# The order of a slot in the first layer's loop: bias rows and the older gradient product first, transposes after the state products

## Chip, cores and metric

The kernel runs on one core of a Trainium2 chip. The metric is the device time of one execution in microseconds, the median of the runs shown. TensorE multiplies matrices and writes PSUM; VectorE and ScalarE compute elementwise and read and write PSUM and SBUF; GpSimd computes elementwise in SBUF only. Each engine takes its instructions strictly in the order written for it, and waits at a semaphore hold up all that stands behind them.

## What is computed

Two transformer layers over 4 sequences of 512 tokens, 128 wide. The change touches the attention part of the first layer only, a test-time-training recurrence: 16 heads of width 64, 8 chunks of 64 tokens, and in each chunk and head

```python
Z1 = xk_c @ W + bb
x_hat = (Z1 - mu) / std
y = g * x_hat + be
gxh = (y - (xv_c - xk_c)) * g
grad_x = (HD * gxh - gxh.sum(-1) - x_hat * (gxh * x_hat).sum(-1)) / (HD * std)
Wn, bn = W - (eta * xk_c).T @ grad_x, bb - (eta * grad_x).sum(-2)
Zq = xq_c @ Wn + bn
out = xq_c + g * ((Zq - mu2) / std2) + be
```

so a chunk needs the weights W and the bias bb that the chunk before has left. Behind it follow the first layer's mixture of experts and the whole second layer, which the change leaves as they are.

## The kernel before

The kernel is written as one stream per engine, with counted semaphores between them. The recurrence is a loop of 38 slots, `for s in range(4 * NC + 6)` (L533 on ScalarE, L821 on VectorE, L1294 on TensorE; GpSimd has its own, L1083). A chunk is four slots: slot s holds chunk s // 4, one half of the heads (s % 4 // 2) and one pair of sequences (s % 2). Slots 0 to 31 compute Z and its gradient; slots 4 to 35 compute Zq of the chunk before, so in slots 4 to 31 both run side by side. I call s % 4 the kind of a slot.

TensorE's parts of a slot, in the words used below: **bias_rows** (L1178) puts the bias into the two PSUM banks that hold Z and Zq; **state_q** and **state** (L1187) add the products of queries and keys with the weights, 64x64 tiles; **XK_** (L1229) transposes the keys into `second_bank`; **target** (L1217, then L1135 to L1137) computes the gradient's constant part into `first_bank`; **bias** (L1250, odd slots only) subtracts two slots' gradients from the bias; **queries** and **keys** (L1135 to L1137) compute a piece of the next chunk's projections, in `second_bank` and `first_bank`; **dW** (L1265) is the gradient product of an earlier slot; **turn** (L1280) transposes normalised Zq of an earlier slot; **att** (L1291) is the output projection, in slots whose number less two has kind 2 or 3, that is in slots of kind 0 and 1.

ScalarE's parts: **squares** (L476) of Z, **squares_q** (L512) of Zq, **deviation** (L481) and **deviation_q** (L517), both square roots, **bias_high** (L507), and the copies out of PSUM **take_xk** (L491), **take_turned** (L524), **take_u** (L486), **take_queries** (L501), **take_att** (L530), **take_keys** (L457).

VectorE's parts: sums of squares (L747, L809), reciprocals (L753, L814), **xhat** (L759), **normed** (L819, the normalised Zq), **bias_low** (L797), **gradient** (L773), **sum_gx** (L779), **sum_gx_xhat** (L791), **centre** (L785), **update** (L804, weights less dW's product). GpSimd's **scaled** (L1055) follows xhat; **rated** (L1081) ends the gradient.

What ties them around the change: Z and Zq have one PSUM buffer each, so bias_rows of slot s + 1 waits for xhat and for normed of slot s (L1172 and L1174) and, every second slot, for bias_low. normed(s) needs deviation_q(s), which stands behind take_queries(s) in ScalarE's order (L537). queries(s) waits until take_xk(s) has emptied `second_bank`. dW has one PSUM buffer, emptied by update. state(s) needs the update of slot s - 4.

Of the kernel before, what the change touches and what calls it, by code (L numbers as in the profile page):

```python
# [63 lines left out]
def build(nc, A, out, const_d, dbg=None):  # L64
    with ExitStack() as ctx:
# [358 lines left out]
        def _(act):  # L424
# [46 lines left out]
            def squares(s):  # L471
                if s in LIVE:
                    act.wait_ge(CHUNK["z_ready"], s + 1)
                    if s >= 4:
                        act.wait_ge(CHUNK["zq_ready"], s - 3)
                    act.activation(by_pair(sqz[:, :]), z_of, ACT.Square).then_inc(CHUNK["z_squared"], 1)  # L476

            def deviation(s):
                if s in LIVE:
                    act.wait_ge(CHUNK["z_sumsq"], s + 1)  # L480
                    act.activation(sm[:, s % 4, 1, :], sm[:, s % 4, 0, :], ACT.Sqrt, bias=C("ttt_eps"), scale=1.0 / HD).then_inc(CHUNK["z_dev"], 1)  # L481

            def take_u(s):
                if s in LIVE:
                    act.wait_ge(CHUNK["u_ready"], s + 1)
                    act.activation(U[:, s % 4, :], first_bank[:, :], ACT.Copy).then_inc(CHUNK["u_taken"], 1)  # L486

            def take_xk(s):
                if s in LIVE:
                    act.wait_ge(CHUNK["xk_ready"], s + 1)  # L490
                    act.activation(XK[:, s % 4, :], second_bank[:, :], ACT.Copy).then_inc(CHUNK["xk_taken"], 1)  # L491

            def take_keys(s):
                if 2 <= s <= 4 * NC - 3:
                    keys((s - 2) % 4, keys_through(s), first_bank)

            def take_queries(s):
                if 2 <= s <= 4 * NC + 1:
                    m = (s - 2) % 4
                    act.wait_ge(CHUNK["queries_ready"], queries_through(s))  # L500
                    act.activation(qT[:, 2 * m:2 * m + 2, :, :].rearrange("p a b c -> p (a b c)"), second_bank[:, :], ACT.Copy).then_inc(CHUNK["queries_taken"], 1)  # L501
# [7 lines left out]
            def squares_q(s):  # L509
                if s in AFTER:  # L510
                    act.wait_ge(CHUNK["zq_ready"], s - 3)
                    act.activation(by_pair(sq2[:, :]), zq_of, ACT.Square).then_inc(CHUNK["zq_squared"], 1)  # L512

            def deviation_q(s):
                if s in AFTER:
                    act.wait_ge(CHUNK["zq_sumsq"], s - 3)
                    act.activation(rq[:, s % 4, 1, :], rq[:, s % 4, 0, :], ACT.Sqrt, bias=C("ttt_eps"), scale=1.0 / HD).then_inc(CHUNK["zq_dev"], 1)  # L517

            def take_turned(s):
                if s in AFTER:  # L520
                    if s == 4:
                        act.wait_ge(wog_ready, 1)
                    act.wait_ge(CHUNK["normed_turned"], s - 3)
                    act.activation(AT[:, s % 4, :], misc[:, :], ACT.Copy).then_inc(CHUNK["turned_taken"], 1)  # L524

            def take_att(s):
                if s in AFTER and s % 4 >= 2:
                    j, g = s // 4 - 1, s % 2
                    act.wait_ge(CHUNK["att_ready"], 2 * j + g + 1)
                    act.activation(attnT[:, :].rearrange("p (b s) -> p b s", b=B)[:, 2 * g:2 * g + 2, j * K:(j + 1) * K],  # L530
                                   misc[:, 0:P].rearrange("p (b s) -> p b s", b=2), ACT.Identity, bias=bo0[:, :]).then_inc(CHUNK["att_taken"], 1)

            for s in range(4 * NC + 6):  # L533
                take_xk(s), take_turned(s - 2), squares(s), squares_q(s), take_u(s)
                if s % 2:
                    bias_high((s - 3) // 2)
                deviation(s), take_queries(s), deviation_q(s), take_att(s - 2), take_keys(s)  # L537
                if s == 0:
                    act.wait_ge(wq_turned, 1)
                    for n in range(2):  # L540
                        act.activation(wqT[:, 4 * n:4 * n + 4, :], bank[n][:, :].rearrange("p (a c) -> p a c", a=4), ACT.Copy).then_inc(wq_turned_taken, 1)
                if s == 1:
                    act.wait_ge(choice_step, 2)
                    act.activation(rkp[:, 1, :], lgt[:, :], ACT.Exp, bias=es[:, 0:1], accum_out=es[:, 1:2]).then_inc(choice_exp, 1)
                if s == 2:
                    act.wait_ge(out_weights, 1)
                    act.activation(Wqo[:, :], misc[:, 0:P], ACT.Copy).then_inc(out_weights_taken, 1)
                    act.activation(bo0[:, :], misc[:, P:P + 1], ACT.Copy).then_inc(out_weights_taken, 1)
                if s == 4:
                    act.wait_ge(ranks_turned, 1)  # L550
                    act.activation(rpT[:, :, :, :], misc[:, :].rearrange("p (k t r) -> p k t r", k=2, t=NT), ACT.Copy).then_inc(ranks_taken, 1)
# [91 lines left out]
        def _(dve):  # L643
# [124 lines left out]
            def gradient(s):  # L768
                if s in LIVE:
                    u = s % 4  # L770
                    dve.wait_ge(CHUNK["scaled_ready"], s + 1)
                    dve.wait_ge(CHUNK["u_taken"], s + 1)
                    dve.tensor_tensor(gx[:, u, :], t1[:, u, :], U[:, u, :], ALU.add).then_inc(CHUNK["gx_ready"], 1)  # L773
# [42 lines left out]
            def normed(s):  # L816
                if s in AFTER:
                    dve.wait_ge(CHUNK["zq_rdev"], s - 3)
                    dve.tensor_tensor(by_pair(Am[:, s % 2, :]), zq_of, per_pair(rq[:, s % 4, 2, :]), ALU.mult).then_inc(CHUNK["normed_ready"], 1)  # L819

            for s in range(4 * NC + 6):  # L821
                centre(s - 1), sum_squares(s), sum_squares_q(s), rdev(s), xhat(s), rdev_q(s)
                if s % 2:
                    bias_low((s - 3) // 2)
                normed(s), rate_of(s - 1), gradient(s), update(s - 2), sum_gx(s), sum_gx_xhat(s)
                if s == 0:
                    choice(0), choice(1)
                elif s == 1:
                    choice(2), choice(3)
                elif s == 2:  # L830
                    choice(4), choice(5)
                elif s == 3:
                    choice(6)
# [291 lines left out]
        def _(pe):  # L1125
# [166 lines left out]
                    pe.matmul(to, Wqo[:, :], xnT[:, :].rearrange("p (b s) -> p b s", b=B)[:, 2 * g:2 * g + 2, j * K:(j + 1) * K], start=False, stop=True, skip_group_check=True).then_inc(CHUNK["att_ready"], 1)  # L1292

            for s in range(4 * NC + 6):  # L1294
                XK_(s), bias_rows(s), state_q(s), state(s), target(s)
                if s % 2:
                    bias((s - 3) // 2)
                queries(s), att(s - 2), keys(s), dW(s - 2), turn(s - 1)
                if s == 0:
                    pe.wait_ge(wg_ready, 1)  # L1300
                    pe.wait_ge(rates_biased, 1)
                    for b in range(B):
                        last = pe.matmul(misc[0:BE, :], wgP[:, b, :], xnT[:, b * S:(b + 1) * S], start=(b == 0), stop=(b == B - 1))
                    last.then_inc(choice_logits, 1)
                    pe.wait_ge(wq_loaded, 16)
                    for a in range(NP):
                        last = pe.transpose(bank[a // 4][:, a % 4 * P:(a % 4 + 1) * P], wq[:, a * P:(a + 1) * P], ident)
                    last.then_inc(wq_turned, 1)
                if s == 2:
                    pe.wait_ge(wo_loaded, 16 * 5)  # L1310
                    pe.wait_ge(wq_turned_taken, 2)
                    pe.wait_ge(choice_step, 1)
                    for a in range(NP):
                        pe.matmul(misc[:, 0:P], wqT[:, a, :], wo[:, a, :], start=(a == 0), stop=(a == NP - 1))
                    for a in range(NP):
                        last = pe.matmul(misc[:, P:P + 1], wo[:, a, :], bet[:, a:a + 1], start=(a == 0), stop=(a == NP - 1))
                    last.then_inc(out_weights, 1)
                if s == 4:
                    pe.wait_ge(ranks_ready, 2)
                    pe.wait_ge(out_weights_taken, 2)  # L1320
                    for k in range(2):
                        for t in range(NT):
                            last = pe.transpose(misc[:, (k * NT + t) * BE:(k * NT + t + 1) * BE], rkp[:, k, t * P:(t + 1) * P], ident[0:BE, 0:BE])
                    last.then_inc(ranks_turned, 1)
# [255 lines left out]
```

## Time and profile before

| | us |
|---|---|
| median of 3 runs (lowest, highest) | 975.94 (974.56, 976.08) |
| the profiled execution, its own time | 973.86 |
| its span in the trace | 971.7 |
| the 38 slots of the loop, roughly | 45 to 327 of the span |
| mean granted TensorE clock | 0.973 of full |

| engine | busy us | share of the span |
|---|---|---|
| TensorE, matmul | 889.8 | 92% |
| VectorE | 786.3 | 81% |
| GpSimd | 626.3 | 64% |
| TensorE, weight load | 618.2 | 64% |
| ScalarE | 556.4 | 57% |

The shares are means over stages with different limits. A matmul's end is modelled, so the busy time of TensorE overlaps itself; the distance from one start to the next is the safer reading.

### The profile page before, as it was taken

How to read it: one execution, taken by the hardware profiler on the slowest of the kernel's cores; microseconds unless marked ns; L12 is line 12 of the kernel's file. 1: busy time of each engine (PE TensorE's matmuls, PEld its weight loads, DVE VectorE, ACT ScalarE, POOL GpSimd, SP SyncE). 2: the span in 40 equal slices, each digit the busy share in tenths (PEclk: the TensorE clock that was granted, in tenths of full speed). 3: DMA queues.
4: the chain of work that ended last, by engine and by line, in shares of the span. 5: the costliest groups of instructions: out<-in, count | busy, mean ns of one | idle time of the engine just before them, and what ended most of it. 6: DMA issues, size and time to landing. Idle time of an engine off the chain costs nothing.

```text
span 971.7 us, 19701 instructions
## 1 busy us (share of the span) xinstructions
PE 889.8 (92%) x7768; PEld 618.2 (64%) x7768; DVE 786.3 (81%) x1182; ACT 556.4 (57%) x828; POOL 626.3 (64%) x571
## 2 busy tenths in 40 slices
PE   1788999999998897799999999999999999999997
PEld 1566778778786677556666656655656666666554
DVE  7768988899886626797888897898788788888876
ACT  3444566666654362456657556666665765656653
POOL 4357888888784002868559559657757855955862
PEclk9888999999999899799999999999999999999999
DMA  8100000000000302101101111101201210220110
GB/s 228 25 2 1 2 3 2 3 2 2 3 3 1 88 2 87 39 38 64 56 12 60 65 27 62 63 4 61 73 25 55 64 47 24 70 75 20 45 52 21
DMA packets 24963, 38.26 MB, mean 39 GB/s; under 512 B 9316, under 2 KB 15480, under 8 KB 22824
## 3 DMA queue, kind: packets, MB, share of 16 engines
q1 hardware_dynamic: 23240, 34.74, 11.7%
q10 hardware_dynamic: 1632, 2.27, 0.7%
q8 instruction: 62, 1.02, 0.4%
q14 instruction: 29, 0.24, 0.1%
HBM read 28.29 MB, written 1.43 MB: 31 GB/s over the span
## 4 chain that ended last, share of the span: by engine, by line
PE 54%; POOL 18%; DVE 13%; issue 8%; ACT 5%; DMA 1%; SPq 0%; POOLq 0%; ACTq 0%; DVEq 0%
PE bank L1135 9%; POOL hdl L1108 8%; PE bank L1137 8%; PE bank L1136 8%; PE bank L1399 5%; POOL hdh L1106 4%; PE bank L1291 3%; PE quad L1187 2%; DVE hdh L954 2%; PE quad L1440 2%; POOL arena L1061 2%; POOL arena L1055 2%; PE quad L1178 2%; PE bank L1250 2%; PE quad L1335 2%
## 5 line engine op out<-in xcount | busy, mean ns | idle before, releaser
L947 DVE TENSOR_REDUCE mx<-quad 128x4 f32<-128x2048 f32 x64 | 146.4, 2287 | 41.3 <-PE quad L1430 41.2
L1106 POOL CAST hdh<-xn 128x512 fp32r<-128x512 f32 x96 | 65.6, 683 | 144.9 <-ACT xn L616 144.9
L631 ACT ACTIVATE ex<-quad 128x2048 f32<-128x2048 f32 x64 | 120.6, 1884 | 51.7 <-PE quad L1440 51.6
L1108 POOL TENSOR_TENSOR hdl<-hd,hdh 128x512 fp32r<-128x512 f32 x96 | 129.5, 1349 | 7.7
L1108 POOL TENSOR_TENSOR hdl<-xn,hdh 128x512 fp32r<-128x512 f32 x96 | 128.4, 1338 | 7.7
L616 ACT ACTIVATE hd<-bank,b1c 128x512 f32<-128x512 f32 x128 | 88.0, 687 | 64.4 <-POOL hdl L1108 30.3
L1135 PE MATMUL bank<-hdh,W2h 128*128 128x512 f32 x256 | 110.9, 433 | 3.0 <-DVE hdl L957 1.5
L616 ACT ACTIVATE xn<-bank,b1c 128x512 f32<-128x512 f32 x128 | 87.9, 687 | 33.9 <-PE bank L1137 16.5
L1137 PE MATMUL bank<-hdl,W2h 128*128 128x512 f32 x256 | 100.5, 393 | 0.0
L1136 PE MATMUL bank<-hdh,W2l 128*128 128x512 f32 x256 | 100.3, 392 | 0.0
L1135 PE MATMUL bank<-cH,W1h 128*128 128x512 f32 x192 | 81.2, 423 | 0.7 <-DVE cL L974 0.7
L1137 PE MATMUL bank<-cL,W1h 128*128 128x512 f32 x192 | 75.8, 395 | 0.0
L1136 PE MATMUL bank<-cH,W1l 128*128 128x512 f32 x192 | 75.6, 394 | 0.0
L1106 POOL CAST hdh<-hd 128x512 fp32r<-128x512 f32 x96 | 69.8, 727 | 0.0
L1135 PEld LDWEIGHTS bank<-hdh,W2h 128*128 128x128 f32 x256 | 47.9, 187 | 33.4 <-issue 12.4
L1399 PE MATMUL bank<-ex,Vx 128*32 128x512 f32 x512 | 65.1, 602 | 0.0
L969 DVE TENSOR_TENSOR cur<-cur,add 128x512 f32<-128x512 f32 x60 | 57.0, 949 | 2.1
L1061 POOL TENSOR_TENSOR arena<-arena 128x512 f32<-128x512 f32 x32 | 41.0, 1280 | 27.2 <-DVE arena L773 27.2
L963 DVE SCALAR_TENSOR_TENSOR add<-bank,b2T,cwB 128x512 f32<-128x512 f32 x64 | 47.7, 746 | 13.1 <-PE bank L1137 12.9
L1055 POOL TENSOR_TENSOR arena<-arena,gg 128x512 f32<-128x512 f32 x32 | 40.8, 1275 | 24.0 <-DVE arena L759 24.0
L1137 PEld LDWEIGHTS bank<-hdl,W2h 128*128 128x128 f32 x256 | 48.0, 188 | 11.2
L1136 PEld LDWEIGHTS bank<-hdh,W2l 128*128 128x128 f32 x256 | 48.2, 188 | 6.7
(301 smaller groups left out, 2200.4 us busy)
## 6 DMA issues: line engine op xcount, KB each, us to landing
cwB<-gate_rows SPq DMA_DIRECT2D x16, 1024.0 KB, 4.7
kx<-kqh SPq DMA_DIRECT2D x32, 64.0 KB, 2.1
qx<-kqh SPq DMA_DIRECT2D x32, 64.0 KB, 2.1
ex<-in_L_ffn_W SPq DMA_DIRECT2D x1, 1024.0 KB, 5.9
kx<-kql SPq DMA_DIRECT2D x16, 64.0 KB, 2.1
qx<-kql SPq DMA_DIRECT2D x16, 64.0 KB, 2.1
rec<-rec_rows SPq DMA_DIRECT2D x32, 32.0 KB, 2.1
out<-fin SPq DMA_DIRECT2D x4, 256.0 KB, 2.3
```

The source lines that it names most:

```text
L616: act.activation(tile(n), bank[TILE_BANK[n % 3]][:, :], ACT.Gelu_apprx_tanh, bias=b1c[:, n:n + 1]).then_inc(ROUND["gelu_ready"], 1)
L631: act.activation(ex[:, t % 2, :, :], quad[:, :, :], ACT.Exp, scale=float(AD) ** -0.5).then_inc(ROUND["exps_ready"], 1)
L947: dve.tensor_reduce(mx[:, t, :], quad[:, :, :], AX_X, ALU.max, negate=True).then_inc(ROUND["score_max"], 1)
L969: dve.tensor_tensor(now, before, add[:, e % 2, :], ALU.add).then_inc(ROUND["cur_added"], 1)
L1055: pool.tensor_tensor(t1[:, u, :], xh[:, u, :], gg[:, 512 * hf:512 * hf + 512], ALU.mult).then_inc(CHUNK["scaled_ready"], 1)
L1061: pool.tensor_tensor(t1[:, u, :], gx[:, u, :], xh[:, u, :], ALU.mult).then_inc(CHUNK["gx_xhat"], 1)
L1106: pool.tensor_copy(hdh[:, m % RING, :], tile(n)).then_inc(ROUND["pool_split"], 1)
L1108: pool.tensor_tensor(hdl[:, m % RING, :], tile(n), hdh[:, m % RING, :], ALU.subtract).then_inc(ROUND["pool_split"], 1)
L1135: pe.matmul(to, lh, rh, start=start, stop=False, skip_group_check=True)
L1136: pe.matmul(to, ll, rh, start=False, stop=False, skip_group_check=True)
L1137: return pe.matmul(to, lh, rl, start=False, stop=stop, skip_group_check=True)
L1399: last = pe.matmul(bank[5][32 * h:32 * h + 32, :], Vx[:, t, QH * r + h, :], ex[:, t % 2, h, :], start=(t == 0), stop=(t == NT - 1), skip_g ...
```

## The change

It permutes calls in the three loops; no instruction is added, removed or resized, and GpSimd's loop stays.

- TensorE: XK_ stood ahead of bias_rows and now stands behind the state products. dW of two slots back stood at the end of the slot; now dW of three slots back stands behind bias_rows, ahead of the state products. turn of one slot back stood at the end; now turn of two slots back stands between the state products and XK_. One slot has thus bias_rows, dW, state_q, state, turn, XK_, target, (bias), queries, att, keys.
- ScalarE: take_xk and take_turned stood ahead of squares, in the order named; now they follow squares and squares_q, take_turned first. deviation moves from behind bias_high to ahead of it.
- VectorE: sum_gx moves ahead of update.

```diff
@@ ScalarE
-                take_xk(s), take_turned(s - 2), squares(s), squares_q(s), take_u(s)
+                squares(s), squares_q(s), take_turned(s - 2), take_xk(s), take_u(s), deviation(s)
                 if s % 2:
                     bias_high((s - 3) // 2)
-                deviation(s), take_queries(s), deviation_q(s), take_att(s - 2), take_keys(s)
+                take_queries(s), deviation_q(s), take_att(s - 2), take_keys(s)
@@ VectorE
-                normed(s), rate_of(s - 1), gradient(s), update(s - 2), sum_gx(s), sum_gx_xhat(s)
+                normed(s), rate_of(s - 1), gradient(s), sum_gx(s), update(s - 2), sum_gx_xhat(s)
@@ TensorE
-                XK_(s), bias_rows(s), state_q(s), state(s), target(s)
+                bias_rows(s), dW(s - 3), state_q(s), state(s), turn(s - 2), XK_(s), target(s)
                 if s % 2:
                     bias((s - 3) // 2)
-                queries(s), att(s - 2), keys(s), dW(s - 2), turn(s - 1)
+                queries(s), att(s - 2), keys(s)
```

## Rows read from the trace of the kernel before

**Rows 1.** The page, part 4: shares of the chain that ended last, by engine.

```profile
PE 54%; POOL 18%; DVE 13%; issue 8%; ACT 5%; DMA 1%; SPq 0%; POOLq 0%; ACTq 0%; DVEq 0%
```

**Rows 2.** Windows: stretch, length, each engine's busy us, granted clock, DMA share, GB/s.

```profile
175.00:200.00 25.00, 25.00 (x473) 20.36 (x472) 22.36 (x41) 15.31 (x33) 20.20 (x17) 1.00 0.01 2
```

**Rows 3.** Timeline, slot 10 (kind 2): start us, length us, engine, line, operation.

```profile
130.43 0.73 PE L1178 MATMUL quad<-Bhl,pair 4*128 4x512 f32 x2
...
131.09 1.16 PE L1187 MATMUL quad<-Wst,arena 64*64 64x64 f32 x64
...
132.18 0.50 PE L1217 MATMUL bank<-gbr,ones 128*128 128x512 f32 x1
132.32 0.60 ACT L476 ACTIVATE arena<-quad 128x512 f32<-128x512 f32 x1 [0.69 <-PE quad L1187]
...
132.81 0.59 ACT L512 ACTIVATE arena<-quad 128x512 f32<-128x512 f32 x1
...
133.21 0.28 PE L1135 MATMUL bank<-xth,wqh 128*128 128x256 f32 x1
...
134.12 0.60 ACT L501 ACTIVATE arena<-bank 128x512 f32<-128x512 f32 x1
...
134.97 0.69 PE L1265 MATMUL quad<-arena 64*64 64x64 f32 x32
...
135.30 0.69 DVE L819 TENSOR_TENSOR arena<-quad,rq 128x512 f32<-128x512 f32 x1
...
135.59 0.66 PE L1280 MATMUL bank<-cst,arena 128*128 128x128 f32 x4
...
136.08 0.60 PE L1229 MATMUL bank<-cst,arena 128*128 128x128 f32 x4
```

**Rows 4.** Timeline, slot 11 (kind 3), and the first row of slot 12.

```profile
136.61 0.73 PE L1178 MATMUL quad<-Bhl,pair 4*128 4x512 f32 x2
...
139.65 1.05 PE L1250 MATMUL bank<-arena,cst 128*32 128x512 f32 x4
...
140.64 0.39 PE L1135 MATMUL bank<-xth,wqh 128*128 128x256 f32 x1
...
141.65 0.60 ACT L501 ACTIVATE arena<-bank 128x512 f32<-128x512 f32 x1
...
143.20 0.68 DVE L819 TENSOR_TENSOR arena<-quad,rq 128x512 f32<-128x512 f32 x1
...
144.02 0.70 PE L1178 MATMUL quad<-Bhl,pair 4*128 4x512 f32 x2
```

**Rows 5.** Timeline, starts of slots 8 and 9 (kinds 0, 1), parts of slot 9.

```profile
113.37 0.70 PE L1178 MATMUL quad<-Bhl,pair 4*128 4x512 f32 x2
...
121.29 0.73 PE L1178 MATMUL quad<-Bhl,pair 4*128 4x512 f32 x2
...
123.04 0.50 PE L1217 MATMUL bank<-gbr,ones 128*128 128x512 f32 x1
...
124.17 1.05 PE L1250 MATMUL bank<-arena,cst 128*32 128x512 f32 x4
...
126.22 0.60 ACT L501 ACTIVATE arena<-bank 128x512 f32<-128x512 f32 x1
...
128.08 0.69 DVE L819 TENSOR_TENSOR arena<-quad,rq 128x512 f32<-128x512 f32 x1
```

**Rows 6.** Timeline, bias_rows of slots 5, 6 and 7, with the wait ahead.

```profile
90.66 0.70 PE L1178 MATMUL quad<-Bhl,pair 4*128 4x512 f32 x2 [0.82 <-DVE arena L819]
...
98.92 0.70 PE L1178 MATMUL quad<-Bhl,pair 4*128 4x512 f32 x2 [0.44 <-DVE arena L819]
...
105.36 0.70 PE L1178 MATMUL quad<-Bhl,pair 4*128 4x512 f32 x2 [0.21 <-DVE arena L819]
```

**Rows 7.** Windows of 1 us about the clock's fall near 298; columns as in group 2.

```profile
296.00:297.00 1.00, 0.12 (x2) 0.00 (x0) 1.00 (x2) 0.60 (x1) 1.00 (x1) 1.00 0.00 0
...
299.00:300.00 1.00, 1.00 (x7) 1.00 (x6) 0.80 (x3) 0.31 (x1) 1.00 (x2) 0.50 0.00 0
```

## Prediction

> **What bounds the kernel now.** I read the page's chain first: TensorE holds 54% of it [rows 1], and only the first layer's loop, some 280 us of the 971.7, is touched. Then the windows of that loop: in 175 to 200 TensorE is busy 25.00 of 25.00 us at full clock [rows 2]. The reader should not stop there, since a queue can be full and yet only just in time. So I read the timeline of four slots, one of each kind. From one bias_rows to the next, slots 8 to 11 take 7.92, 9.14, 6.18 and 7.41 us (113.37, 121.29, 130.43, 136.61, 144.02), together 30.65 [rows 3 to 5]. The start-to-start distances in slot 10 add up without a hole: TensorE's work sets these slots.
>
> The second thing to read is when VectorE's normed comes, because bias_rows of the next slot waits for it. In slot 10 normed starts at 135.30; bias_rows can follow a normed's start by 0.82 (143.20 to 144.02 in slot 11, where it was indeed waited for), so from 136.12; it starts at 136.61 [rows 3, 4]. The margin is 0.49 us in kind 2 and nothing in kind 3. And before the loop settles, the wait is plain: bias_rows of slots 5, 6 and 7 stood idle 0.82, 0.44 and 0.21 us, released by normed [rows 6]. So this is a loop in balance: TensorE's work on one side, and on the other the chain bias_rows, products, target, (bias), queries, take_queries, deviation_q, reciprocal, (bias_low), normed, next bias_rows. What kept the chain covered is that dW, turn and XK_ stood behind keys, between the last step that the chain needs and the bias_rows that waits for it.
>
> **The change part by part.** TensorE's three moved parts, from slot 10: dW takes 0.62 (134.97 to 135.59), turn 0.49, XK_ 0.53 (136.08 to 136.61 of slot 11) [rows 3, 4]. Together 1.64 us leave the stretch where TensorE did useful work while normed was under way, and enter the stretch between bias_rows and queries, on which normed depends. Their work is the same; their place lengthens the chain by what they take and removes the cover by the same amount.
>
> For dW next to the state products the trace has no row. Bounds: 0.62 as it stands, or at the products' own rate, 64 matmuls in 1.09 us (131.09 to 132.18), so 32 in 0.55 [rows 3]. I take 0.55, because both groups are 64x64 tiles with the same count of columns; a saving of 0.07 a slot. The Trainium skill (TensorEngine Tiling (Array Packing), Key Properties) says that changing the tiling mode drains TensorE, which speaks for this change, as dW and the products would share one change of mode. The rows allow no more than that 0.07 for it.
>
> The chain by kind, with T = 0 at bias_rows. The products start at 0.66 + 0.55 = 1.21 (bias_rows takes 0.66, 130.43 to 131.09), turn at 2.30, XK_ at 2.79, target at 3.32 [rows 3].
>
> ScalarE next. squares starts 0.14 after the products give way (132.18 to 132.32), so at 2.44; ScalarE starts one such operation every 0.49 (132.32 to 132.81), so squares_q is at 2.93, take_turned 3.42, take_xk 3.91, done with 0.60 at 4.51 [rows 3]. queries may start about 0.09 later, 4.60, while TensorE is ready at 3.32 + 1.03 = 4.35 (132.18 to 133.21) [rows 3]. This is an added wait: 0.25 in even slots, with queries, att, keys queued behind it; in odd slots bias fills it. Bounds 0 to 0.25; I take 0.25, since it follows from ScalarE's order.
>
> Kind 2: queries 4.60, take_queries 0.91 later (133.21 to 134.12) at 5.51, normed 1.18 later (134.12 to 135.30) at 6.69, next bias_rows 0.82 later: **7.51** against 6.18 [rows 3, 4].
>
> Kind 3: bias at 3.32 + 1.13 = 4.45 (123.04 to 124.17; in slot 11 it waited for GpSimd's rated, which is long done now), queries 0.99 later (139.65 to 140.64) at 5.44, take_queries 1.01 later at 6.45, normed 1.55 later (141.65 to 143.20) at 8.00, next bias_rows: **8.82** against 7.41 [rows 4, 5]. The upper bound of the step from take_queries to normed is slot 9's 1.86 (126.22 to 128.08) [rows 5]; there xhat lay in between on VectorE. Now deviation stands ahead of bias_high, xhat is out of the way by then, and I take 1.55.
>
> Kind 0: att (about 1.9 us) stands behind queries and covers the chain of 7.51. TensorE's own work remains: 7.92 less 0.07 plus 0.25, **8.10**. Kind 1: 9.14 less 0.07, **9.07**; its chain of 8.82 is covered.
>
> The rest I cost at nothing. deviation(s) now follows take_u(s), which waits for a target that comes 1.6 us later; it starts at about 5.1 and xhat ends at about 6.4, ahead of normed in both kinds, so what hides it is the chain itself. If that cover went, xhat and then normed would move by the difference. update(s) waits for a dW behind bias_rows; sum_gx fills that on VectorE, and three slots remain until the weights are needed. take_xk and take_turned held nobody up. DMA: no transfer is issued in the loop's body. The first slots 0 to 4 are set by VectorE (its long selection of experts' tokens sits there), so the longer TensorE stretch hides. In slots 32 to 35 no keys and no target are left: dW and turn only change slots.
>
> Sum: four slots 33.50 against 30.65, so +2.85, six times for slots 8 to 31: 17.1. Slots 5, 6 and 7 took 8.26, 6.44 and 8.01 (90.66, 98.92, 105.36, 113.37) [rows 5, 6] and become 8.82, 7.51, 8.82: +2.4. Together **+19.5 us**: span 971.7 to 991.2, the profiled execution 973.86 to 993.4, and, since that execution lies 2.08 under the median, the median 975.94 to **995.4**.
>
> Own range of this case. Low: no wait for take_xk, giving 7.85, 9.07, 7.26 and 8.82, so +2.35 a period, 14.1 and 2.1 for slots 5 to 7: 992.1. High: dW at 0.62 and 1.86 before normed in odd slots, giving 8.17, 9.20, 7.58 and 9.20, so +3.5 a period, 21.0 and 3.3: 1000.2.
>
> **The rivals.**
>
> A. TensorE's work is all that counts (the other side). If normed comes early enough in spite of the longer way, slots remain set by TensorE, whose work is unchanged but for the 0.07 a slot, 32 times: 2.2 us, so 973.7. The skill's rule on the drain named above would be its reason and could make it more. It decides from the point where the chain of kind 2 is under 6.1 and that of kind 3 under 7.3. For it: busy 25.00 of 25.00 [rows 2]. Against: zero margin in slot 11 and waits in slots 5 to 7 [rows 4, 6].
>
> B. The clock falls. At 296 TensorE was idle for most of a microsecond, with smaller holes in the 7 us before, and from 299 to 302 it was granted 0.50, that is 1.2 in place of 2.4 GHz [rows 7]. The case above opens holes of 1.3 to 1.5 us in kinds 2 and 3 of every period. If each period then has one stretch of about 3.2 us at half clock, and half of it is lost on TensorE's path (1.6 us), seven periods cost 11 more: 1006.6. Against: slots 5 and 6 had holes of 0.82 and 0.44 and kept full clock.
>
> C. The chain shortens elsewhere. deviation ahead of bias_high and ScalarE's free time let normed come about 0.5 us sooner than I put it in kinds 2 and 3 (13 slots), and the wait for take_xk vanishes (7 slots by 0.25): 8.3 less, 987.1.
>
> **How the numbers follow.** The main case 0.54 (992 to 1000), A 0.10 (of which 0.07 faster, 0.03 within the bound), B 0.22 (1000 to 1010), C 0.14 (978 to 992, 0.01 of it within the bound). A measurement of this kernel tells 0.2%, about 2 us, from no change. So faster 0.07, same 0.04, slower 0.89. For the range, A falls outside and so does a part of C: 984 to 1010 holds about 8 in 10.
>
> **What would show it.** Right: in the middle of the loop TensorE's busy share drops to about 90%, bias_rows of kinds 3 and 0 (behind slots of kind 2 and 3) show idle time of about 1.3 and 1.4 us released by normed L819, none of that size ahead of kinds 1 and 2, and a period of 33.5 us between equal kinds. dW to the products: 0.55. queries of even slots start 4.6 us after bias_rows. B: granted clock 0.5 in some 1 us windows between 115 and 290. Wrong: a period of 30.7 or less (A), or holes released by anything other than normed, such as xhat or update, which would mean that I missed the wait that ends last.

## The result, and the profile after

| | before | changed |
|---|---|---|
| median, us (lowest, highest) | 975.25 (974.42, 976.08) | 1000.99 (997.88, 1002.24) |
| profiled execution, us | 973.86 | 1001.21 |
| its span, us | 971.7 | 999.1 |
| mean granted clock | 0.973 | 0.957 |

The ratio is 1.0253, with a 95% interval of 1.0234 to 1.0272: 25.7 us slower where 995.4 was forecast. The page's engine shares and the chain by engine, to be held against [rows 1]:

```profile
PE 891.0 (89%) x7768; PEld 624.2 (62%) x7768; DVE 783.0 (78%) x1182; ACT 551.1 (55%) x828; POOL 625.7 (63%) x571
...
PE 56%; POOL 14%; DVE 13%; issue 8%; ACT 7%; DMA 1%; SPq 0%; POOLq 0%; ACTq 0%; DVEq 0%
```

The busy times are those of before within 2 us for TensorE and 6 for any engine. Nothing got more expensive; the time is waiting. Where, is told by the windows (slot 11, then a piece of slot 12) and by the view of waits over 120 to 300 us. Columns of windows as in [rows 2]; a line of waits gives engine, its line, the releaser, total us, times, longest. PE is TensorE's matmuls, PEld its weight loads.

```profile
141.00:150.00 9.00, 6.82 (x126) 4.92 (x127) 7.67 (x16) 4.63 (x10) 6.81 (x6) 1.00 0.01 2
152.50:155.00 2.50, 2.50 (x26) 2.34 (x19) 2.24 (x4) 1.79 (x4) 2.42 (x3) 0.53 0.00 0
```

```profile
PE quad L1178 <- DVE arena L819: 14.6, 10, 1.7
...
PEld bank L1135 <- ACT arena L491: 14.1, 19, 0.8
...
PEld quad L1178 <- DVE Bhl L797: 9.4, 5, 1.9
...
PE bank L1135 <- ACT arena L491: 1.6, 7, 0.2
```

TensorE, 25.00 of 25.00 us busy in [rows 2], has holes now. bias_rows (L1178) waits for normed (L819) and for bias_low (L797), and queries (L1135) for take_xk (L491). A weight load counts as idle while matmuls ahead of it still run, so the two PE lines are the ones that give lost time: the 9.4 us of PEld behind bias_low lie in the same holes as PE's wait for normed (ahead of slot 12, 1.88 and 1.70 us), and normed, which stands behind bias_low on VectorE, ends last. In the view of before over the same stretch the wait for normed came twice, 0.4 us and, ahead of slot 32, 1.2 us, and the wait for take_xk not at all. The timeline of slot 10, which answers [rows 3]:

```profile
134.16 0.70 PE L1178 MATMUL quad<-Bhl,pair 4*128 4x512 f32 x2
...
134.79 0.69 PE L1265 MATMUL quad<-arena 64*64 64x64 f32 x32
...
135.30 1.11 PE L1187 MATMUL quad<-Wst,arena 64*64 64x64 f32 x64
...
136.34 0.66 PE L1280 MATMUL bank<-cst,arena 128*128 128x128 f32 x4
...
136.84 0.60 PE L1229 MATMUL bank<-cst,arena 128*128 128x128 f32 x4
...
137.19 0.48 PE L1217 MATMUL bank<-gbr,ones 128*128 128x512 f32 x1
...
137.93 0.62 ACT L491 ACTIVATE arena<-bank 128x512 f32<-128x512 f32 x1
...
138.60 0.39 PE L1135 MATMUL bank<-xth,wqh 128*128 128x256 f32 x1 [0.23 <-ACT arena L491]
...
139.61 0.60 ACT L501 ACTIVATE arena<-bank 128x512 f32<-128x512 f32 x1 [0.40 <-PE bank L1137]
...
140.66 0.69 DVE L819 TENSOR_TENSOR arena<-quad,rq 128x512 f32<-128x512 f32 x1
...
141.50 0.70 PE L1178 MATMUL quad<-Bhl,pair 4*128 4x512 f32 x2 [1.22 <-DVE arena L819]
```

Read it downwards as the chain: TensorE reaches queries 4.44 us after bias_rows, where it was 2.78 in [rows 3]; take_queries, normed and the next bias_rows hang on it, and TensorE idles 1.22. Slot 11, answering [rows 4], does the same and ends in a hole of 1.70:

```profile
145.65 1.05 PE L1250 MATMUL bank<-arena,cst 128*32 128x512 f32 x4
...
146.63 0.39 PE L1135 MATMUL bank<-xth,wqh 128*128 128x256 f32 x1
...
147.65 0.60 ACT L501 ACTIVATE arena<-bank 128x512 f32<-128x512 f32 x1 [0.31 <-PE bank L1137]
...
149.20 0.68 DVE L819 TENSOR_TENSOR arena<-quad,rq 128x512 f32<-128x512 f32 x1
...
150.02 0.70 PE L1178 MATMUL quad<-Bhl,pair 4*128 4x512 f32 x2 [1.70 <-DVE arena L819]
```

The holes have a second price. In the windows above the clock granted from 152.5 to 155 is 0.53, that is mostly 1.2 GHz in place of 2.4. Four of the six slots of kind 0 in the loop's middle (8, 12, 16, 20) take 9.15 us, the other two 8.09 and 8.08; slot 31 takes 11.49 where its kind takes 8.52. Slot 6 is at half clock too, from 100 to 103, and takes 8.53 where its kind takes 7.34.

Where the difference of the two spans lies, by the starts of bias_rows and of the last att:

| stretch | before | changed | more |
|---|---|---|---|
| up to slot 5 | 90.66 | 90.74 | 0.1 |
| slots 5 to 7 | 22.71 | 25.42 | 2.7 |
| slots 8 to 31 | 183.95 | 203.98 | 20.0 |
| of these: full clock, six periods of 32.80 for 30.65 | | | 12.9 |
| of these: half clock, 4 times 1.06, and 2.97 in slot 31 | | | 7.2 |
| slots 32 to the last att | 27.35 | 29.98 | 2.6 |
| from there to the first hidden activation of layer two | 73.52 | 72.79 | -0.7 |
| the second layer | 573.5 | 576.2 | 2.7 |

The 2.7 us of slots 5 to 7 hold 1.2 us of half clock in slot 6. The 2.7 us of the second layer lie in code that the change doesn't touch. In the traces of the twelve experiments the same code takes 573.3 to 575.8 us and does not follow the length of the slots, so this row is scatter between executions; it is part of why this profiled pair differs by 27.4 and the medians by 25.7.

### The profile page after: what moved, and what is told of

Same layout as the page of the kernel before. It is cut to its first block, busy times and chain, and to the rows that moved or that the text cites. A ratio compares the mean times of both kernels' runs of the same rounds, so it can differ in the third digit from the quotient of the medians.

```text
span 999.1 us, 19701 instructions
## 1 busy us (share of the span) xinstructions
PE 891.0 (89%) x7768; PEld 624.2 (62%) x7768; DVE 783.0 (78%) x1182; ACT 551.1 (55%) x828; POOL 625.7 (63%) x571
## 4 chain that ended last, share of the span: by engine, by line
PE 56%; POOL 14%; DVE 13%; issue 8%; ACT 7%; DMA 1%; SPq 0%; POOLq 0%; ACTq 0%; DVEq 0%
PE bank L1135 10%; POOL hdl L1108 8%; PE bank L1137 8%; PE bank L1136 8%; PE bank L1399 5%; POOL hdh L1106 4%; PE quad L1187 3%; PE bank L1291 3%; PE quad L1178 2%; PE quad L1265 2%; PE quad L1440 2%; PE bank L1280 2%; PE quad L1430 2%; PE quad L1335 2%; ACT ex L631 2%
## 5 line engine op out<-in xcount | busy, mean ns | idle before, releaser
L1135 PE MATMUL bank<-hdh,W2h 128*128 128x512 f32 x256 | 110.8, 433 | 2.4 <-DVE hdl L957 1.5
L1135 PE MATMUL bank<-cH,W1h 128*128 128x512 f32 x192 | 81.2, 423 | 0.7 <-DVE cL L974 0.7
L1135 PEld LDWEIGHTS bank<-hdh,W2h 128*128 128x128 f32 x256 | 47.9, 187 | 32.7 <-issue 12.4
L476 ACT ACTIVATE arena<-quad 128x512 f32<-128x512 f32 x32 | 19.1, 598 | 80.5 <-PE quad L1187 80.5
L1178 PE MATMUL quad<-Bhl,pair 4*128 4x512 f32 x72 | 27.4, 462 | 36.1 <-DVE arena L819 28.2
L963 DVE SCALAR_TENSOR_TENSOR add<-bank,b2T,cwB 128x512 f32<-128x512 f32 x64 | 47.7, 746 | 13.1 <-PE bank L1137 12.9
```

The costliest lines, as they stand in the source:

```text
L963: dve.scalar_tensor_tensor(out=add[:, e % 2, :], in0=bank[6 if e % 2 else 4][:, :], scalar=b2T[:, e:e + 1], in1=cwB[:, e, :], op0=ALU.add, ...
L1135: pe.matmul(to, lh, rh, start=start, stop=False, skip_group_check=True)
L1178: pe.matmul(quad[:, 2 + h, :].rearrange("p (q a c) -> p q a c", q=2, a=4), pair[r, :], rows[:, h].unsqueeze(1).broadcast_to([4, 2, 4, HD]) ...
```

## The experiments

Every kernel's slot lengths are read off its own timeline as distances of bias_rows starts, full-clock slots of the middle. This table is the measure of all runs:

| kernel | kind 0 | 1 | 2 | 3 | period | median us |
|---|---|---|---|---|---|---|
| before | 7.92 | 9.14 | 6.18 | 7.41 | 30.65 | 975.3 |
| changed | 8.09 | 8.85 | 7.34 | 8.52 | 32.80 | 1001.0 |
| e1, dW alone | 7.65 | 9.31 | 6.31 | 8.01 | 31.28 | 981.3 |
| e2, transposes with ScalarE | 8.23 | 8.95 | 6.90 | 8.05 | 32.13 | 989.2 |
| e3, ScalarE and VectorE alone | 9.24 | 9.27 | 7.25 | 7.39 | 33.15 | 991.9 |
| e4, changed, holes filled | 8.06 | 8.85 | 7.35 | 8.51 | 32.77 | 991.3 |
| e5, changed, deviation_q first | 8.07 | 8.79 | 7.02 | 7.62 | 31.50 | 982.5 |
| e6, changed, take_xk first | 7.60 | 8.85 | 7.01 | 8.51 | 31.97 | 995.7 |
| e7, dW ahead of bias_rows | 7.84 | 9.47 | 6.04 | 7.78 | 31.13 | 978.9 |
| e8, e7 with keys ahead of att | 8.79 | 9.71 | 6.04 | 7.78 | 32.32 | 985.3 |
| e9, e5 and e6 together | 7.59 | 8.79 | 7.04 | 7.62 | 31.04 | 979.8 |
| e10, both roots ahead of take_u | 7.60 | 8.79 | 6.56 | 8.02 | 30.97 | 983.9 |
| e11, e10, sums ahead of centre | 7.59 | 8.79 | 6.68 | 7.78 | 30.84 | 982.1 |
| e12, one dW in four moved | 7.18 | 9.61 | 6.18 | 7.41 | 30.38 | 974.5 |

**One part of the change at a time (e1, e2, e3).** The theory was the balance of the prediction; the rivals were that TensorE's work alone counts, and that one single part carries the loss.

e1:

```diff
-                XK_(s), bias_rows(s), state_q(s), state(s), target(s)
+                XK_(s), bias_rows(s), dW(s - 3), state_q(s), state(s), target(s)
-                queries(s), att(s - 2), keys(s), dW(s - 2), turn(s - 1)
+                queries(s), att(s - 2), keys(s), turn(s - 1)
-                gradient(s), update(s - 2), sum_gx(s)
+                gradient(s), sum_gx(s), update(s - 2)
```

> Only dW moves (three slots back, behind bias_rows), with VectorE's sum_gx ahead of update; turn, XK_ and ScalarE's order stay as before. Theory (balance of work and chain): in the changed kernel dW and the products run 0.15 us shorter a slot than before (dW 0.62 to 0.52, products 1.09 to 1.04), and the chain from bias_rows to normed grows by 0.52. Kinds 0 to 3: 7.8, 9.0, 6.2 and 7.75 against 7.92, 9.14, 6.18 and 7.41, together about 30.7 against 30.65, so 975 to 978 us. Rival (only TensorE's work counts): 0.15 less in each of some 30 slots, 971 us. Rival (dW's new place is the cause of the whole loss): 995 or more.

981.33 us, ratio 1.0055 (1.0039 to 1.0072), above the 975 to 978 expected. Kinds 0 and 2 came within 0.15 of the expectation; 3 and 1 came longer by 0.26 and 0.31. For kind 1 the timeline shows a wait that I had not listed: with dW gone from between keys and the transposes, XK_ of the next slot stands waiting for take_keys.

```profile
130.18 0.66 PE L1229 MATMUL bank<-cst,arena 128*128 128x128 f32 x4 [0.23 <-ACT arena L457]
...
131.42 0.69 PE L1265 MATMUL quad<-arena 64*64 64x64 f32 x32
...
131.94 1.11 PE L1187 MATMUL quad<-Wst,arena 64*64 64x64 f32 x64
...
132.98 0.51 PE L1217 MATMUL bank<-gbr,ones 128*128 128x512 f32 x1
```

The same rows show the gain that is real: dW 0.52 and the products 1.04. In kind 0, where att covers everything, the slot is 0.27 shorter.

Outside the table, slots 19 and 20 of this trace are 1.3 and 1.2 us longer than their kinds, at full clock; TensorE stands still there for 1.57 and 0.89 us without a releaser in the profile, so the cause is open.

e2:

```diff
-                XK_(s), bias_rows(s), state_q(s), state(s), target(s)
+                bias_rows(s), state_q(s), state(s), turn(s - 2), XK_(s), target(s)
-                queries(s), att(s - 2), keys(s), dW(s - 2), turn(s - 1)
+                queries(s), att(s - 2), keys(s), dW(s - 2)
```

and ScalarE in the order of the change.

> turn and XK_ go behind the state products and ScalarE follows as in the change; dW and VectorE stay as before. Theory: the chain grows by the two transposes (about 0.85) and in even slots queries waits some 0.4 us for take_xk. Kinds 0 to 3: 8.15, 9.0, 6.9 and 8.0, together +1.4 a period, about 985 us. Rival (the transposes carry the whole loss): 1000 us. Rival (TensorE's work alone): 972 us.

989.24 us, ratio 1.0134 (1.0119 to 1.0149). Each kind is within 0.08 us of what the chain gave. The total is 4 us above the 985 expected; slots 5 and 31, both partly at half clock, are 2.7 and 1.6 us longer than slot 5 of before and slots of kind 3 here. The hole ahead of slot 11 has the releaser that it should:

```profile
140.40 0.46 PE L1178 MATMUL quad<-Bhl,pair 4*128 4x512 f32 x1 [0.60 <-DVE arena L819]
```

e3 takes ScalarE's and VectorE's orders of the change, and TensorE's of before.

> TensorE's order as before; ScalarE and VectorE in the order of the change. Theory: take_xk is now done only about 4.0 us after bias_rows while TensorE is ready for queries at 2.8, so in even slots queries and all behind it wait 1.2 us; in odd slots bias covers all but 0.2. Kinds 0 and 2 grow by 1.2 each, 1 and 3 by 0.2: +2.8 a period, about 995 us, with idle time of TensorE ahead of L1135 released by ACT L491, and none from normed. Rival (ScalarE's order costs nothing, it merely follows): 975 us.

991.85 us, ratio 1.0164 (1.0148 to 1.0179).

```profile
137.55 0.62 ACT L491 ACTIVATE arena<-bank 128x512 f32<-128x512 f32 x1
...
138.22 0.38 PE L1135 MATMUL bank<-xth,wqh 128*128 128x256 f32 x1 [1.06 <-ACT arena L491]
```

take_xk had its input ready from the slot's start and was done last; TensorE idled 1.06 us for it. ScalarE's new order "follows" only if TensorE's transposes come late too. e3's period is the longest of all, but it takes 9 us less than the changed kernel. Of these, 5.2 us lie in slots 8 to 31 (198.75 us for 203.98), where it has no half-clock stretch; the rest lies outside. So no single part carries the loss: each costs alone, and dW alone least.

**Are the holes free, and do they pull the clock down (e4)?**

```diff
                 queries(s), att(s - 2), keys(s)
+                if s % 4 >= 2 and 6 <= s < 4 * NC:
+                    pe.wait_ge(CHUNK["state_updated"], s - 2)
+                    for _ in range(9):
+                        pe.matmul(quad[:, 0, 256:512], wkh[:, 0:P], tokens(xth, 0), start=True, stop=True, skip_group_check=True)
```

The wait is one that the next dW makes anyway.

> The changed kernel with nine more matmuls (about 0.116 us each, 1.04 us together, the shape of those of keys, into a part of PSUM that nobody reads) behind keys in every slot of kind 2 and 3 from slot 6 on. Theory: TensorE is idle there for 1.2 to 1.7 us waiting for normed, so the work fits in at no cost: kinds 2 and 3 stay 7.34 and 8.52. If the holes are also what makes the granted clock fall, the half-clock stretches in slots 8, 12, 16 and 20 (1.06 us each) and in slot 31 (about 3) go, and the kernel takes 994 us; if not, 1001. Rival (TensorE's work sets these slots): 14 times 1.04 more, 1015 us.

991.32 us, ratio to before 1.0155 (1.0138 to 1.0172), against 1.0253 for the changed kernel: more work, 10 us less. By the two traces 7.4 us of it lie in slots 8 to 31 (196.62 for 203.98) and 2.3 between slot 32 and the last att. The filler's row, the bias_rows behind it, and the window that was at 0.53 above:

```profile
140.25 1.23 PE L1302 MATMUL quad<-xth,wkh 128*128 128x256 f32 x9
...
141.63 0.46 PE L1178 MATMUL quad<-Bhl,pair 4*128 4x512 f32 x1 [0.15 <-DVE arena L819]
```

```profile
152.50:155.00 2.50, 2.28 (x15) 1.75 (x15) 2.28 (x4) 2.50 (x6) 2.42 (x3) 1.00 0.00 0
```

The filler costs nothing: kinds 2 and 3 keep their length to 0.01 us. All six slots of kind 0 are now at 8.06, and slot 31 at 8.52. This settles two things: kinds 2 and 3 are set by the chain and not by TensorE's work, and TensorE's idling there is what the half clock followed from. The mean granted clock of e4's four executions is 0.971 to 0.979, that of the changed kernel's 0.957 to 0.964. Slots 5 and 6, which end before the first filler can act, still have half-clock stretches in e4.

**What sits in the chain (e5, e6, e9).** The changed kernel, with ScalarE's order edited. e5:

```diff
-                take_queries(s), deviation_q(s), take_att(s - 2), take_keys(s)
+                deviation_q(s), take_queries(s), take_att(s - 2), take_keys(s)
```

> The changed kernel with deviation_q ahead of take_queries on ScalarE, which takes queries and its copy out of normed's chain. Theory: in the changed kernel's trace deviation_q of slot 10 could start at 139.2 in place of 140.10 and normed then follows xhat at about 140.3 in place of 140.66; in slot 11 deviation_q at 147.25 in place of 148.14 and normed at 148.35 in place of 149.20. Kinds 2 and 3 go from 7.34 and 8.52 to 7.0 and 7.7, kind 1 from 8.85 to about 8.7, kind 0 stays at 8.06 and loses its half-clock stretches as the holes shrink: about 986 us against 1001. Rival (normed is held up by VectorE's own work or by bias, not by ScalarE's order): no change, 1001 us.

982.48 us, ratio 1.0068 (1.0053 to 1.0083). Kinds 2 and 3 came to 7.02 and 7.62, expected 7.0 and 7.7. Of slots 8 to 31 only slot 31 had a half-clock stretch (9.16 us, 1.5 over its kind).

```profile
134.86 0.30 ACT L517 ACTIVATE rq<-rq,cst 128x8 f32<-128x8 f32 x1
...
136.08 0.69 DVE L819 TENSOR_TENSOR arena<-quad,rq 128x512 f32<-128x512 f32 x1
...
136.92 0.70 PE L1178 MATMUL quad<-Bhl,pair 4*128 4x512 f32 x2 [0.88 <-DVE arena L819]
```

deviation_q no longer waits for queries, and normed comes when xhat is through. One swap of two calls returns 18.5 of the 25.7 us. In slots 8 to 31 it returns 13.4: 7.8 by the shorter chain (1.30 a period) and 5.7 by half clock that did not come.

e6:

```diff
-                squares(s), squares_q(s), take_turned(s - 2), take_xk(s), take_u(s), deviation(s)
+                squares(s), squares_q(s), take_xk(s), take_turned(s - 2), take_u(s), deviation(s)
```

> The changed kernel with take_xk ahead of take_turned on ScalarE. Theory: queries of even slots waited 0.23 us for take_xk, which now starts 0.49 us sooner, so kinds 0 and 2 go from 8.06 and 7.34 to 7.85 and 7.1, odd kinds stay; 13 times 0.23, and the half-clock stretches stay: 998 us against 1001. Rival (the wait is no part of the loss): 1001 us with kinds 0 and 2 unchanged.

995.69 us, ratio 1.0200 (1.0183 to 1.0218). Even kinds fell by 0.49 and 0.33, more than the 0.23 that the row of slot 10 names. That idle time is counted from a modelled end of the matmul ahead; from start to start, target's 1.03 would have put queries at 4.06 after bias_rows and it stood at 4.44, a wait of 0.38. The first matmul behind the wait then took 0.22 (138.60 to 138.82) where in before it takes 0.12; together that is about the 0.49 of kind 0. Four slots of kind 0 still took 9.13 to 9.15.

e9 has both edits.

> The changed kernel with both ScalarE edits: take_xk ahead of take_turned, and deviation_q ahead of take_queries. TensorE and VectorE as in the change. Theory (two separate delays of one chain): kind 0 falls to 7.6 (from the first), kinds 1 and 3 to 8.8 and 7.6 (from the second), kind 2 to 7.0 or, if both delays count there, 6.8; together 31.0 or less against 30.65 before, no half-clock stretch: 976 to 979 us. Rival (the two edits remove the same wait): as with deviation_q first alone, 982 us.

979.76 us, ratio 1.0043 (1.0030 to 1.0057), 0.8 above the range expected; slot 27 did have a half-clock stretch (9.17 us, 1.55 over its kind). Kinds 0, 1, 3 took each edit's gain; kind 2 stayed at 7.04. There the two removed the same time, and take_u, then deviation, then xhat ended last.

**Cutting target out of the chain (e10, e11).** e10:

```diff
-                squares(s), squares_q(s), take_turned(s - 2), take_xk(s), take_u(s), deviation(s)
+                squares(s), squares_q(s), take_xk(s), take_turned(s - 2), deviation(s), deviation_q(s), take_u(s)
-                take_queries(s), deviation_q(s), take_att(s - 2), take_keys(s)
+                take_queries(s), take_att(s - 2), take_keys(s)
```

> The changed kernel with ScalarE's order squares, squares_q, take_xk, take_turned, deviation, deviation_q, take_u, bias_high, take_queries, take_att, take_keys: neither root waits for a copy that needs target or queries. Theory: the chain no longer contains target and queries, so what the change put ahead of them (turn, XK_) costs nothing, and the shorter TensorE time remains. In the trace with deviation_q first, slot 10's sums of squares end at 133.8 and 134.4, so both roots are done by 134.9 in place of 135.2, the xhat starts at 134.3 in place of 135.25, and normed about 0.8 sooner: kind 2 about 6.2; kind 3 7.35, kinds 0 and 1 7.6 and 8.6. Together 29.8 against 30.65: 968 to 971 us, faster than the kernel before. Rival (TensorE's way through the longer stretch itself is the loss, whatever ScalarE does): 976 or more.

983.93 us, ratio 1.0084 (1.0071 to 1.0098): my expectation fell. Kind 2 gained, to 6.56 and not 6.2; kind 3 lost, 8.02 for 7.62; and the loop's first slots lost 5.2 us (slot 5 starts at 94.96, in e9 at 89.78). Slot 8 was at half clock (9.16 us). Both losses have a row, the first two lines from slot 2, the third from slot 7:

```profile
66.15 0.30 ACT L481 ACTIVATE sm<-sm,cst 128x8 f32<-128x8 f32 x1 [3.31 <-DVE sm L747]
...
66.99 0.58 PE L1135 MATMUL bank<-xth,wkh 128*128 128x256 f32 x1 [3.10 <-ACT arena L486]
```

```profile
117.09 0.74 DVE L797 SCALAR_TENSOR_TENSOR Bhl<-Bhl,cst,bank 36x512 fp32r<-36x512 f32 x1 [0.39 <-ACT Bhl L507]
```

In slot 2 VectorE is busy selecting experts' tokens; a root that waits for it now holds up take_u, and so keys on TensorE. In odd slots bias_high stands behind both roots and take_u, and bias_low waits for it.

e11 also puts sum_squares and sum_squares_q ahead of centre on VectorE.

> The run above, and on VectorE both sums of squares ahead of centre, which in slots of kind 3 stood in front of them for 0.9 us. Theory: in kind 3 the roots come up to 0.8 us sooner, but bias_low and normed are then held by bias_high (bias ends about 5.1 us after bias_rows), so kind 3 gains 0.1 to 0.3 at most, while GpSimd's less, which needs centre, comes later: 966 to 971 us. Rival (GpSimd's chain becomes the bound): 3 us or more above the run above.

982.05 us, ratio 1.0065 (1.0052 to 1.0078), missed as well. Kind 3 gained 0.24 and kind 2 lost 0.12. Over e9 to e11 the two kinds together take 14.66, 14.58 and 14.46 us, whatever is put first; before, they took 13.59. What bounds them jointly in these three was not isolated.

**Where TensorE's shorter time comes from, and whether it can be kept (e7, e8, e12).**

e7 is the kernel before with dW between XK_ and bias_rows.

```diff
-                XK_(s), bias_rows(s), state_q(s), state(s), target(s)
+                XK_(s), dW(s - 3), bias_rows(s), state_q(s), state(s), target(s)
-                queries(s), att(s - 2), keys(s), dW(s - 2), turn(s - 1)
+                queries(s), att(s - 2), keys(s), turn(s - 1)
```

> The kernel before with dW moved by three places only: behind turn and XK_ and just ahead of bias_rows, so that it stands outside the stretch from bias_rows to queries, and still close to the 64x64 products. ScalarE and VectorE as before. Theory: the chain does not grow, the cover stays; the shorter TensorE time that the changed kernel showed comes from the order of tile shapes, so about 0.1 less in kinds 0 and 2, while XK_ right behind turn waits some 0.3 us for take_keys in kind 1 as it did with dW behind bias_rows. 974 to 977 us. Rival (only direct neighbourhood of dW and the products saves time): kinds 0 and 2 unchanged or longer, 977 or more.

978.85 us, ratio 1.0031 (1.0019 to 1.0043), above the 974 to 977 expected. Kinds 0 and 2 are 0.08 and 0.14 shorter, kind 1 is 0.33 longer, with the wait for take_keys that e1 had (2.6 us over 11 slots in both). Kind 3 is 0.37 longer, which I had not expected.

e8 puts keys ahead of att, and take_keys ahead of take_att.

> The order of the run above, with keys ahead of att on TensorE and take_keys ahead of take_att on ScalarE. Theory: XK_'s wait for take_keys in kind 1 is then hidden under att (1.9 us), so kind 1 is at most 9.05 and the kernel 972 to 974 us. Rival (the wait was not the reason for kind 1's length): as the run above.

985.29 us, ratio 1.0098 (1.0081 to 1.0115), a miss. turn now comes right behind att and needs the bank that take_att is still emptying:

```profile
PE bank L1280 <- ACT attnT L530: 6.6, 12, 0.6
```

e12:

```diff
-                XK_(s), bias_rows(s), state_q(s), state(s), target(s)
+                XK_(s), bias_rows(s)
+                if s % 4 == 1:
+                    dW(s - 3)
+                state_q(s), state(s), target(s)
-                queries(s), att(s - 2), keys(s), dW(s - 2), turn(s - 1)
+                queries(s), att(s - 2), keys(s)
+                if s % 4:
+                    dW(s - 2)
+                turn(s - 1)
```

with sum_gx ahead of update in slots of kind 0.

> The kernel before with one of four dW moved: the one at the end of kind 0 goes behind bias_rows of kind 1, with sum_gx ahead of update on VectorE in kind 0 only. att covers the chain in both kinds, and no XK_ comes to stand behind a take_keys that it needs. Theory: the run with dW alone moved had kind 0 at 7.65 against 7.92, where TensorE is the bound, made up of dW 0.52 for 0.63, products 1.04 for 1.10, keys 0.80 for 0.89, turn 0.46 for 0.49; the same is saved once a period here, kinds 0 and 1 together 16.8 against 17.06, kinds 2 and 3 unchanged at 13.58: 973.5 us, 0.2% under the kernel before. Rival (the order of kinds 2 and 3 hangs on VectorE's timing in 0 and 1, so something is lost there): 976 to 978.

974.53 us, ratio 0.9991 (0.9982 to 1.0000). The period is 30.38 for 30.65: kinds 0 and 1 give 16.79 for 17.06 as worked out, kinds 2 and 3 are untouched. That is all of the change's idea that these experiments made usable. In the median it is 0.9 us, half of what seven periods give, and the interval reaches 1: the best version found, but not surely faster than the kernel before.

## Why the prediction was right, point by point

- **What bounds.** A loop in balance between TensorE's work and the chain to normed: right. The holes stand ahead of the slots named, with L819 as releaser, and TensorE's busy share of the loop (116 to 320) fell from 97% to 90%, as forecast. The holes are 1.22 and 1.70 us, forecast 1.3 and 1.4; those were differences of slot lengths, and with the terms for dW and take_xk the prediction's own sum gives 1.15 and 1.48. Run e4 shows that the holes are free for work, and e5 that ScalarE's order behind queries is part of the chain.
- **The chain's steps.** Forecast 4.60 after bias_rows for queries in kind 2, measured 4.44; take_queries 5.51, measured 5.45; normed 6.69, measured 6.50; next bias_rows 7.51, measured 7.34. Kind 3: 8.82, measured 8.52. Kind 0: 8.10, measured 8.09, but by luck: e6, which removes the wait for take_xk, has 7.60, so TensorE's own time fell by 0.32 where I had 0.07, and the wait cost 0.49 where I had 0.25. Kind 1: 9.07, measured 8.85, and it was the chain that ended last there: normed starts at 133.32, 0.84 ahead of bias_rows. Rival A is out.
- **Term mis-sized: TensorE's shorter time.** I allowed 0.07 a slot for dW next to the products. In the timelines of before and changed, slots 8 to 11, dW falls from 0.62 to 0.51, the products from 1.09 to 1.04, and XK_ followed by target takes 0.35, where followed by bias_rows it took 0.53. In e1 keys lose 0.09 and turn 0.03 as well. So 0.3 a slot and more, and the period came out at 32.80, not 33.50: I had 4.2 us too much over six periods. In kind 3 target starts 3.04 after bias_rows (forecast 3.32), and every later step of the chain keeps that lead. The Trainium skill's sentence that changing the tiling mode drains TensorE (TensorEngine Tiling (Array Packing), Key Properties) points the right way and was under-weighed: e1 with all dW next to the products has 0.27 less in kind 0, e7 with dW next to bias_rows only 0.08. That it is the drain, and not another effect of neighbouring shapes, no run shows.
- **The clock, rival B.** I gave it a chance of its own, and it happened in part: 7.2 us in slots 8 to 31, and 1.2 in slot 6, where I had priced 11. By the time alone, 1001.0 lies in the band given to B (1000 to 1010, 0.22) and not in that of the main case (992 to 1000, 0.54). The half clock is the larger reason why 1001 stands above 995. The counter-argument I gave, that slots 5 and 6 kept full clock with holes of 0.82 and 0.44, was weak, since the new holes are one and a half to four times as long.
- **Costed at nothing, wrongly: the tail.** It took 2.6 us more from slot 32 to the last att, and only a part of that is the order's. Slots 33 and 34, at full clock in both kernels, took 7.00 and 4.62 us for 6.38 and 4.18. Then, turn of slot 34 had stood in slot 35 and now stands in slot 36, right behind turn of slot 33, whose result ScalarE must first take away (take_turned ends at 341.72, turn starts at 341.82; the profile names no releaser). The last-but-one att starts 5.22 us after the last bias_rows (338.37) where it was 3.75 (314.85 to 318.60), part of it at half clock. But e4 has the same order there and takes 27.69 us for this stretch, 0.3 more than before, and 1.1 of what it saves lie in slot 32, which it runs at full clock (5.47 us for 6.61): about 7 us of e4's tail are at half clock and about 14 of the changed kernel's. How much the order costs there by itself, apart from the 1.1 us of slots 33 and 34, is not isolated.

```profile
341.82 1.09 PE L1280 MATMUL bank<-cst,arena 128*128 128x128 f32 x4 [0.73 <-issue]
...
343.59 1.65 PE L1291 MATMUL bank<-arena,wog 128*128 128x128 f32 x6 [0.69 <-ACT arena L524]
```

- **Costed at nothing, rightly:** the first slots (0.1 us), update behind dW, the transfers. **Rival C**, a chain shortened elsewhere, did not come by itself; e5 and e6 show what it would have taken.

So the sum was 0.7 a period too high, and 7.2 us of half clock and 2.6 of tail were missing from it: 19.5 - 4.2 + 7.2 + 2.6 = 25.1 against 25.7 measured. That 995.4 came as near as 5.6 us is in part luck, since an error of 4.2 one way stood against 9.8 the other. In slots 5 to 7 it is the same: +2.7 for +2.4, made of two slots 0.5 and 0.3 shorter than forecast and one 1.0 longer, at half clock.

## What to carry to other kernels

A queue that is busy all the time may still be covering a chain that is exactly as long. Before moving work from behind the last step that a chain needs to ahead of it, count the work twice: it lengthens the chain and it leaves the cover. When an order is changed on one engine, look at each copy that another engine makes: a copy out of a shared bank belongs where its consumer's wait ends, and here the position of one square root and one copy on a half-idle ScalarE was worth 21 of the 26 us lost, the half clock that went with the holes included.

## What the runs showed of the hardware

- TensorE's granted clock fell from 2.4 to 1.2 GHz behind holes of 1.2 and 1.7 us that were 7 us apart (the changed kernel, slots 10 to 12), and did not in that place when 1.04 us of matmuls was put into each hole (e4). It did not fall there in every period: kind 0 ran at full clock in slots 24 and 28. In e3 a hole of 1.06 us in every second slot left it at full clock from slot 8 to slot 31, while in e9 it fell once, in slot 27, behind a hole of 1.09.
- The start-to-start time of the same matmuls depended on what stood next to them: 32 64x64 matmuls took 0.62 us between wide ones (before) and 0.51 ahead of more of their own shape (changed); four transposes took 0.53 ahead of bias_rows' 4-row matmuls and 0.35 ahead of 128-row ones.
- Idle time of TensorE in the profile is counted from a modelled end: a wait shown as 0.23 us was 0.38 from start to start (changed kernel, slot 10).
